# New places for the steps of every engine in a fused attention and mixture-of-experts kernel

## The chip, the cores and the metric

The kernel runs on one core of a Trainium2 chip. The time is that of the device, in microseconds (us), as the median of several executions. Matrix products run on TensorE (PE), whose weight loads have rows of their own (PEld); VectorE is DVE, ScalarE is ACT, GpSimd is POOL, and SP is the SyncE queue that issues nearly all DMAs. Everything is fp32.

## What is computed

Two results are added to the input `x` of 4 batches of 1024 tokens and 128 channels. The first is a power attention with 16 query heads over 8 key and value heads of size 64: squared scores take the place of the exponential, with a decay by token.

```python
q = _rope(qkvg[..., :hq*d]); k = _rope(...); v = ...
log_G = jnp.repeat(jnp.cumsum(jax.nn.log_sigmoid(6.906768 + gate), axis=1), 2, axis=2)
logits = 2 * jnp.log(jnp.abs(s) + 1e-30) + log_G[:, :, :, None] - log_G[:, :, None, :]
logits = jnp.where(tril, logits, -inf); a = jnp.exp(logits - logits.max(-1))
y = a @ v / (a.sum(-1) + 1e-6); y = layernorm(y, over d) * ln_w; out = y @ w_proj
```

The second is a layer norm followed by a router with 7 experts (the best two of each token, 366 places for each expert), a shared feed-forward network of width 512 for all tokens, and the experts' networks on the gathered tokens, added back with their weights.

## The kernel before

The work is cut into 32 pairs: 4 batches times 8 key heads, each with its two query heads. A pair has ten score steps (`STEPS`), in four diagonal units w = 0 to 3 (`ORDER` = 0, 2, 1, 3) of 256 columns. A score step is a set of PE products into two banks of PSUM (L778); DVE scales the diagonal ones with a masked decay block (`diagonal`, L1361), ACT squares the others (L964), DVE takes the running maximum over keys (`maximum`, here "top": L1380, L1390, L1392, L1397), ACT weighs the blocks (L960) and PE multiplies with the values (L811). Expert pairs are 9, 12, 15, ..., 27; there the gathered tokens of one expert run through up (PE, L614/L617 or their kin), gate and down.

No engine decides its order at run time. Each order is written out by tables:

- `*_FIRST` for the setup: a row (kind, at, by, then, na, nb) stands for na x nb items, item (a, b) at the tick at + by * a + then * b; `spread` (L89) sorts them.
- `*_AT` for the steady loop: a row (tick, kind, i) is placed in each pair p at T0 + 20 * p + tick if `wanted` (L133) allows it; `agenda` (L152) sorts them. A negative tick therefore lies before the pair, beside the work of the pair ahead. Scatters, loads and stores have tables of their own (`SCATTER_AT` and others).

Ticks are no times: they only fix which instruction follows which on an engine. What an engine waits for is fixed by semaphores at each step and does not depend on the tables. `jobs_of` (L179) hands PE's side jobs out in batches of five score steps: scores first, then transposes (`FLIPS`), then the other side jobs, then the value products. `bank_plan` (L185) walks through that order and gives each job the PSUM bank that has been taken least recently.

The steps that follow are named by kind:

- DVE setup: norm (layer norm), `forget` (the logarithms of the decay gates and their sums), `route` (L1162 to L1264: choice of the two experts, places, weights; among them the prefix sums of the experts' counts by doubling shifts, L1208 copy and L1209 add), gate (L1280, product of silu and the second up product), add (L1285).
- DVE loop: scale, top, fold (L1406, L1408: the maximum over the key blocks), sum (L1415, L1417), var (L1422, L1424), root (L1432 to L1440: an inverse square root by thirteen small steps), sup and sdn (L1318, L1326: the shared network of the last two units of tokens, in pair 31), wp (L1313: projection added to acc).
- POOL: `k` and `q` (`rotate`, L1502 and L1505, the rotation of keys and queries, after SP's swap of halves), `vs` (`scale_values`, L1516: values times decay, for the units w = 1, 2, 3 of the pair with 256, 128 and 384 columns; the trace calls the first two U and the third VS), `select` (L1524: masks the decay block), `scatter` (L1534, an indirect DMA), `combine` (L1544), n1 (L1570) and n2 (L1574), which divide and norm the outputs.
- ACT: decay (L882: the decay block that select masks), square, weigh, k, q and v copies (L897, L892, L905), y (L912), fin (L918), nt (L975), ysq (L985), silu (L844), e1 (L864: the exponential of the router), ht (L838).
- SP: swapk and swapq (L473), row (L448), keys (L491), rows (L502), weights (L455 to L462), sload (L521).

The exponential of e1 and the silu of the shared network use different tables of ACT, so going from one to the other takes an ACT_TABLE_LOAD. Here are the routing's last steps on DVE; the step behind e1 waits for it, and `gk` releases the scatters on POOL.

```python
v.tensor_tensor(e1, M12[:, 1], M12[:, 0], ALU.subtract).then_inc(v_e1, 1)   # L1251
yield
ve.wait_ge(a_e1, 1)
chain(v.tensor_scalar(e2, e1, 1.0, None, ALU.add))
...
v.tensor_tensor(gk[:, :], e1, keep[:, 32:64], ALU.mult).then_inc(v_gk, 1)   # L1264
```

Of the kernel before, what the change touches and what calls it, by code (L numbers as in the profile page):

```python
# [1639 lines left out]
```

## Time and profile before

| | us |
|---|---|
| median of 3 runs | 1023.90 |
| lowest and highest | 1023.67, 1024.99 |
| profiled execution | 1027.59 |
| its span | 1025.50 |
| PE busy in the span | 964.1 (94%) |
| DVE busy | 881.6 (86%) |
| ACT busy | 678.0 (66%) |
| POOL busy | 628.7 (61%) |

The busy time of an engine is the time in which it works, not in which it waits. The windows view cuts the span into stretches and gives each engine's busy time there. In the timeline view a row is an instruction (or some of one kind in a row); the bracket at its end says how long the engine had been idle and what ended that. PE does 8871 matmuls, DVE 1730 instructions, ACT 1078 and POOL 593.

### The profile page before, as it was taken

To read this page: it belongs to the slowest core of one execution; us is meant where nothing else is said; L and a number is where in the kernel's file an instruction comes from. 1 tells how busy PE (TensorE), PEld (TensorE's weight loads), DVE (VectorE), ACT (ScalarE), POOL (GpSimd) and SP (SyncE) were. 2 spreads that over 40 slices of the span, in tenths; PEclk is the share of its full clock that TensorE was granted. 3 is DMA by queue.
4 is the path that set the end of the run, shared out by engine and by line. 5 is a ranking of instruction groups with operands and counts; after the bars stand their busy time and mean duration, and the time that the engine had idled before them with its cause. 6 is when DMAs were issued, how large, how long until landed. Compare 5 with 4: busy or idle time off the path is not lost.

```text
span 1025.5 us, 23347 instructions
## 1 busy us (share of the span) xinstructions
PE 964.1 (94%) x8871; PEld 709.2 (69%) x8871; DVE 881.6 (86%) x1730; ACT 678.0 (66%) x1078; POOL 628.7 (61%) x593
## 2 busy tenths in 40 slices
PE   3999788989898999999999999999999999999977
PEld 2675466666676767676777686777677777767755
DVE  5668759999999988999998998899898989899983
ACT  2243466757667667868777868777876867786731
POOL 0320568898989775657567575748566747665611
PEclk9999989999999999999999999999999999999999
DMA  9301225443434343445354454345345435444550
GB/s 268 97 1 47 57 80 135 100 119 89 119 87 103 97 128 90 104 120 126 84 132 119 104 135 118 94 121 132 81 117 127 111 92 132 98 103 102 136 143 21
DMA packets 78767, 109.44 MB, mean 107 GB/s; under 512 B 15901, under 2 KB 47005, under 8 KB 78528
## 3 DMA queue, kind: packets, MB, share of 16 engines
q1 hardware_dynamic: 73584, 105.28, 39.3%
q0 software_dynamic: 5072, 2.67, 1.9%
q8 instruction: 70, 1.15, 0.5%
q14 instruction: 41, 0.34, 0.1%
HBM read 32.40 MB, written 11.36 MB: 43 GB/s over the span
## 4 chain that ended last, share of the span: by engine, by line
PE 71%; DVE 15%; POOL 4%; issue 4%; ACT 3%; DMA 1%; SPq 1%; DVEq 0%; POOLq 0%; ACTq 0%
PE PS L778 20%; PE PS L571 19%; PE PS L811 17%; PE PS L566 6%; DVE PS L1397 2%; PE PS L614 2%; DVE PS L1390 2%; PE PS L617 2%; DVE U L1397 2%; PE PS L624 1%; POOL xe_d L1534 1%; POOL U L1502 1%; DVE SM L1422 1%; PE PS L587 1%; DVE PS L1392 1%
## 5 line engine op out<-in xcount | busy, mean ns | idle before, releaser
L778 PE MATMUL PS<-Qt,Kt 64*128 64x256 f32 (+1 forms) x2560 | 281.0, 369 | 21.0 <-POOL Qt L1505 12.8
L778 PEld LDWEIGHTS PS<-Qt,Kt 64*128 64x128 f32 x2560 | 232.0, 190 | 62.3 <-POOL Qt L1505 14.7
L964 ACT ACTIVATE U<-PS 128x1024 f32<-128x1024 f32 x144 | 141.3, 1023 | 70.7 <-PE PS L778 59.4
L1502 POOL TENSOR_TENSOR U<-U,consts 128x512 f32<-128x512 f32 x96 | 127.3, 1326 | 45.6 <-DMA U<-U 45.5
L811 PE MATMUL PS<-U 128*64 128x256 f32 (+1 forms) x1344 | 141.2, 349 | 0.2 <-ACT U L960 0.2
L811 PEld LDWEIGHTS PS<-U 128*64 128x64 f32 x1344 | 94.0, 137 | 40.4 <-issue 6.0
L1524 POOL TENSOR_SCALAR_AFFINE_SELECT U<-U 128x256 f32<-128x256 f32 x128 | 59.9, 545 | 99.7 <-ACT U L882 99.4
L1570 POOL TENSOR_TENSOR U<-U,SM 128x1024 f32<-128x1024 f32 x32 | 71.7, 2241 | 73.5 <-DVE SM L1417 72.7
L1361 DVE SCALAR_TENSOR_TENSOR U<-PS,U 128x768 f32<-128x768 f32 x96 | 88.6, 953 | 30.8 <-PE PS L778 29.0
L1397 DVE SCALAR_TENSOR_TENSOR PS<-U,ES,PS 128x512 f32<-128x512 f32 x144 | 108.3, 752 | 4.7
L882 ACT ACTIVATE U<-U,negG 128x256 f32<-128x256 f32 (+1 forms) x256 | 98.7, 454 | 9.0 <-DMA U<-H_d 8.2
L1574 POOL TENSOR_TENSOR U<-U,SM 128x1024 f32<-128x1024 f32 x32 | 61.8, 1932 | 60.9 <-DVE SM L1440 60.8
L571 PE MATMUL PS<-XT,W 128*64 128x512 f32 x384 | 94.1, 603 | 0.0
L960 ACT ACTIVATE U<-U 128x768 f32<-128x768 f32 x96 | 81.2, 847 | 16.9 <-DVE U L1361 16.9
L1505 POOL TENSOR_TENSOR Qt<-Qt,U 128x512 f32<-128x512 f32 x64 | 83.6, 1307 | 9.2
L1534 POOL DMA_INDIRECT xe_d<-U,idx_s x64 | 70.1, 1096 | 21.7 <-issue 12.4
L566 PE MATMUL PS<-consts,U 128*128 128x128 f32 x533 | 78.5, 281 | 5.2 <-DVE U L1361 4.1
L566 PEld LDWEIGHTS PS<-consts,U 128*128 128x128 f32 x533 | 58.9, 142 | 20.9 <-issue 11.4
L892 ACT ACTIVATE U<-PS 128x512 f32<-128x512 f32 x64 | 38.1, 597 | 47.7 <-PE PS L571 47.7
L811 PE MATMUL PS<-U,VS 128*64 128x256 f32 x576 | 68.8, 379 | 0.1
L985 ACT ACTIVATE U<-U 128x1008 f32<-128x1008 f32 x32 | 33.4, 1043 | 49.3 <-PE PS L571 25.3
L571 PE MATMUL PS<-Wp,U 128*64 128x128 f32 x1024 | 58.9, 273 | 4.9 <-ACT U L918 4.9
(189 smaller groups left out, 1896.9 us busy)
## 6 DMA issues: line engine op xcount, KB each, us to landing
G<-U SPq DMA_DIRECT2D x512, 64.0 KB
U<-U SPq DMA_DIRECT2D x192, 128.0 KB
U<-H_d SPq DMA_DIRECT2D x32, 512.0 KB
Kt<-Kt SPq DMA_DIRECT2D x32, 256.0 KB
U<-in_w SPq DMA_DIRECT2D x21, 256.0 KB
acc<-in_x SPq DMA_DIRECT2D x4, 512.0 KB, 5.8
ye_d<-G SPq DMA_DIRECT2D x4, 512.0 KB, 7.3
U<-ye_d SPq DMA_DIRECT2D x4, 512.0 KB, 5.2
```

The lines of the kernel that those rows point to most:

```text
L566: return te.transpose(to, src, ident)
L571: mm = te.matmul(to[lo:lo + 64], weights[:, lo:lo + 64], moving, start=start, stop=stop)
L778: mm = te.matmul(bank[:, 256 * n:256 * n + 256 - lo], Kt[u % 2][(ki + hd) % 2][rows, 128 * j:128 * j + 128], Qt[p % 2][m // 2][rows, 256 * ...
L811: mm = te.matmul(P[4][64 * hd:64 * hd + 64, c + lo:c + 256], vt, A[s % NA][:, o:o + 256 - lo], start=begins and n == 0, stop=ends and n == 1)
L882: ex = s.activation(D[un % 3][:, lo:hi], HR[:, 256 * m + 128 * k2:256 * m + 256], ACT.Exp, scale=0.5, bias=negG[:, n:n + 1])
L960: s.activation(a_, a_, ACT.Square).then_inc(a_sd, 1)
L964: s.activation(A[n % NA], PS[:, first:first + 1024], ACT.Square, scale=0.125, bias=GUARD).then_inc(a_so, 1)
L1361: v.scalar_tensor_tensor(A[s % NA].rearrange("p (a t) -> p a t", a=2)[:, :, 0:384], PS[:, first:first + 1024].rearrange("p (a t) -> p a t" ...
L1397: v.scalar_tensor_tensor(run if i == m and n == 1 else PRUN, a_[:, :, n], es, PRUN, ALU.mult, ALU.max).then_inc(v_mx, 1)
L1502: g.tensor_tensor(sw, sw, sinT[:, cols], ALU.mult).then_inc(made, 1)
L1505: g.tensor_tensor(to, to, sw, ALU.add).then_inc(added, 1)
L1534: g.indirect_dma_start(xe_d[:, :], bass.IndirectOffsetOnAxis(ap=idx_s[:, c:c + 1], axis=0), hn_v[:, k], None, bounds_check=NE * SLOT - 1, ...
```

## The change

The tables `PE_FIRST`, `ACT_FIRST`, `DVE_FIRST`, `POOL_FIRST`, `PE_AT`, `ACT_AT`, `DVE_AT`, `POOL_AT` and `SP_AT` get new ticks. No instruction, wait, tile or size changes, and `SCATTER_AT`, `GATES_AT`, `LOAD_AT`, `ADD_AT` and `STORE_AT` stay. Through `bank_plan` 16 of 728 bank choices change. Sorted, the new tables differ from the old ones in this:

- POOL loop: vs1 goes from between vs3 and the rotations to right before vs2, in 31 pairs. Before: select3, vs3, vs1, k1, q0, combine or scatter, n1, q1, vs2, three selects, k0, n2. After: select3, vs3, k1, q0, combine or scatter, n1, q1, vs1, vs2, three selects, k0, n2. One scatter or combine goes before q0 in some pairs.
- ACT loop: decay3 behind weigh1 and v1's copy, nt0 before weigh2, in 32 pairs; ysq of pair 31 behind sup4.
- DVE loop: up6 before q0 in seven expert pairs, sup4 before the last root step of pair 31, else as before.
- SP loop: rows2 before keys in 15 pairs, weights0 behind rows2 and swapk, load 3 before rows(31,0), sload behind rows(31,1).
- PE loop: down before k0 and k1 in three expert pairs; in the tail sup8 earlier, sdn0 before sup14, sup15 behind the fins of pair 31, wp(15,0) before sdn1.
- Setup: on PE ht(0,0) before gate(0,1), cn behind v1, q0 behind down(4,1), q1 behind up(5,3); on ACT v0 before k1, silu(5,3) before e1; on DVE norms earlier among the gates, k0 behind step 12 of route, k1 and add(3) behind step 18, inside the prefix sums of the counts, gate(5,1) from before L1245 to behind it; on POOL vs(0,0) behind the two selects.

The diff's entries that these lines name, one to a line; the rest are left out:

```diff
 PE_FIRST = [
-    ('ht', 32.16, 28.14, 5.08, 4, 2),
+    ('ht', 31.98, 28.12, 5.08, 4, 2),
-    ('rt', 41.4, 27.8, 1.12, 4, 2),
+    ('rt', 40.86, 26.97, 0.83, 4, 2),
-    ('up', 33.04, 24.16, 6.2, 6, 4),
+    ('up', 32.15, 24.16, 7.29, 6, 4),
-    ('cn', 162.68, 0, 0, 1, 1),
+    ('cn', 163.91, 0, 0, 1, 1),
-    ('k', 147.14, 4.08, 0, 2, 1),
+    ('k', 149.42, 2.73, 0, 2, 1),
-    ('q', 167.45, 4, 0, 2, 1),
+    ('q', 171.58, 11.09, 2.19, 2, 1),
-    ('v', 159.28, 4.43, 0, 2, 1),
+    ('v', 158.39, 2.35, 0.57, 2, 1),
...
 ACT_FIRST = [
-    ('ht', 37.33, 28.36, 3.36, 4, 2),
+    ('ht', 35.41, 28.36, 3.36, 4, 2),
-    ('silu', 39.95, 23.79, 6.11, 6, 4),
+    ('silu', 39.95, 23.67, 6.11, 6, 4),
-    ('e1', 172.32, 0, 0, 1, 1),
+    ('e1', 181.04, 0, 0, 1, 1),
-    ('k', 151.74, 4.33, 0, 2, 1),
+    ('k', 153.39, 4.33, 1.27, 2, 1),
-    ('v', 163.14, 3.92, 0, 2, 1),
+    ('v', 157.07, 2.57, 0, 2, 1),
...
 DVE_FIRST = [
-    ('norm', 4.77, 29.15, 0.82, 4, 30),
+    ('norm', 3.71, 24.39, 0.82, 4, 30),
-    ('gate', 39.97, 24.16, 6.28, 6, 4),
+    ('gate', 40.64, 24.16, 6.28, 6, 4),
-    ('add', 83.46, 24.04, 0, 6, 1),
+    ('add', 88.41, 24.22, 0.17, 6, 1),
-    ('forget', 117.51, 0.77, 0, 44, 1),
+    ('forget', 119.82, 0.77, 0, 44, 1),
-    ('route', 149.17, 0.64, 0, 52, 1),
+    ('route', 149.17, 0.64, 0.1, 52, 1),
-    ('k', 153.48, 3.98, 0, 2, 1),
+    ('k', 156.88, 3.98, 0, 2, 1),
-    ('q', 187.97, 4.31, 0, 2, 1),
+    ('q', 180.15, 4.23, 0, 2, 1),
...
 POOL_FIRST = [
-    ('select', 294.1, 6.18, 0, 2, 1),
+    ('select', 254.64, 7.09, 1.48, 2, 1),
-    ('vs', 278.5, 0, 0, 1, 1),
+    ('vs', 275.84, 0, 0, 1, 1),
-    ('k', 159.29, 8.22, 0, 2, 1),
+    ('k', 151.2, 10.61, 0, 2, 1),
-    ('q', 232.63, 8.35, 0, 2, 1),
+    ('q', 237.21, 15.68, 3.36, 2, 1),
...
 PE_AT = [
-    (40.8, 'sup', 8),
+    (33.21, 'sup', 8),
-    (41.4, 'sup', 14),
+    (42.83, 'sup', 14),
-    (41.5, 'sup', 15),
+    (54.33, 'sup', 15),
-    (58.3, 'fin', 1),
+    (59.37, 'fin', 1),
-    (59.31, 'wp', 0),
+    (57.94, 'wp', 0),
-    (54.32, 'down', 0),
+    (50.37, 'down', 0),
...
 ACT_AT = [
-    (10.31, 'decay', 3),
+    (11.47, 'decay', 3),
-    (12.8, 'nt', 0),
+    (12.82, 'nt', 0),
-    (12.4, 'weigh', 2),
+    (13.04, 'weigh', 2),
...
 DVE_AT = [
-    (34, 'root', 0),
+    (33.41, 'root', 0),
-    (37.4, 'root', 2),
+    (37.07, 'root', 2),
-    (38.6, 'sdn', 0),
+    (39.28, 'sdn', 0),
-    (49.0, 'sdn', 1),
+    (40.49, 'sdn', 1),
...
 POOL_AT = [
-    (1.22, 'select', 3),
+    (0.1, 'select', 3),
-    (-16.1, 'vs', 1),
+    (-6.3, 'vs', 1),
-    (3.66, 'vs', 3),
+    (3.81, 'vs', 3),
-    (38.34, 'n2', 0),
+    (37.25, 'n2', 0),
-    (-15.9, 'k', 1),
+    (-15.04, 'k', 1),
-    (-15.66, 'q', 0),
+    (-13.54, 'q', 0),
...
 SP_AT = [
-    (9.68, 'rows', 2),
+    (7.9, 'rows', 2),
-    (-11.27, 'keys', 0),
+    (-12.05, 'keys', 0),
-    (-10.6, 'weights', 0),
+    (-7.61, 'weights', 0),
...
```

## Rows read from the trace of the kernel before

**Rows 1.** Windows view of five stretches, all engines: us and count; then clock, DMA share, GB/s.

```profile
0.00:21.90 21.90, 6.36 (x28) 5.59 (x28) 14.56 (x85) 3.28 (x5) 0.19 (x4) 1.00 0.96 267
21.90:131.50 109.60, 99.14 (x534) 65.64 (x534) 73.20 (x258) 41.44 (x65) 31.08 (x39) 0.98 0.22 57
131.50:375.00 243.50, 224.50 (x2081) 166.97 (x2083) 222.41 (x363) 161.68 (x260) 202.10 (x197) 0.97 0.41 105
375.00:950.00 575.00, 572.90 (x5726) 425.79 (x5724) 516.57 (x919) 439.42 (x702) 371.51 (x340) 1.00 0.44 112
950.00:1025.50 75.50, 61.17 (x508) 45.22 (x504) 54.83 (x107) 32.18 (x49) 23.80 (x17) 0.97 0.37 100
```

**Rows 2.** Timeline of the front: start, duration, engine, line; in brackets idleness and what ended it.

```profile
21.91 2.08 PE L614 MATMUL PS<-U 128*128 128x512 f32 x2 [0.87 <-ACT U L838]
```

**Rows 3.** Timeline of the setup's end, four engines.

```profile
102.03 0.59 ACT L905 ACTIVATE U<-PS 128x504 f32<-128x504 f32 x1 [2.15 <-PE PS L571]
...
103.33 1.27 POOL L1502 TENSOR_TENSOR U<-U,consts 128x512 f32<-128x512 f32 x1 [33.57 <-DMA U<-U]
103.39 1.73 DVE L1209 TENSOR_TENSOR U<-U 128x480 f32<-128x480 f32 x1
...
115.23 0.68 DVE L1280 TENSOR_TENSOR U<-U,PS 128x512 f32<-128x512 f32 x1
116.23 0.23 ACT L864 ACTIVATE SM<-SM 128x32 f32<-128x32 f32 x1 [3.86 <-DVE SM L1251]
116.48 1.28 ACT L844 ACT_TABLE_LOAD   x1
...
131.58 0.80 PE L778 MATMUL PS<-Qt,Kt 64*128 64x256 f32 x2 [6.36 <-POOL Qt L1505]
```

**Rows 4.** Timeline of DVE and POOL around 165, and one maximum at 222.

```profile
164.98 3.57 DVE L1390 SCALAR_TENSOR_TENSOR PS<-U,ES 128x512 f32<-128x512 f32 x1
...
165.34 0.85 POOL L1516 TENSOR_TENSOR VS<-U,ES 128x384 f32<-128x384 f32 x1
...
166.13 0.63 POOL L1516 TENSOR_TENSOR U<-U,ES 128x256 f32<-128x256 f32 x1
166.72 1.27 POOL L1502 TENSOR_TENSOR U<-U,consts 128x512 f32<-128x512 f32 x1
...
222.46 1.71 DVE L1390 SCALAR_TENSOR_TENSOR PS<-U,ES 128x512 f32<-128x512 f32 x1
```

**Rows 5.** Source view of L1390: ns min/median/max; L1397 of DVE's lines, 131.5 to 375.

```profile
L1390 DVE SCALAR_TENSOR_TENSOR PS<-U,ES x64: 696/746/3569, 142.3 to 977.2; 128x512 f32<-128x512 f32 x64
...
L1397 DVE SCALAR_TENSOR_TENSOR PS<-U,ES,PS 128x512 f32<-128x512 f32 x41 | 30.9, 753 | 1.6
```

**Rows 6.** Timeline of ACT, POOL and DVE around select3 and top1 of pair 2.

```profile
189.14 0.79 ACT L882 ACTIVATE U<-U,negG 128x256 f32<-128x256 f32 x2
...
189.83 0.58 ACT L905 ACTIVATE U<-PS 128x504 f32<-128x504 f32 x1
...
190.01 0.50 POOL L1524 TENSOR_SCALAR_AFFINE_SELECT U<-U 128x256 f32<-128x256 f32 x1 [0.95 <-ACT U L882]
...
190.30 0.84 ACT L960 ACTIVATE AX<-AX 128x768 f32<-128x768 f32 x1
...
191.57 1.77 DVE L1390 SCALAR_TENSOR_TENSOR PS<-U,ES,AX 128x512 f32<-128x512 f32 x1
```

**Rows 7.** Timeline of decay and select, in a K rotation's pair and in an expert's pair.

```profile
214.70 0.79 ACT L882 ACTIVATE U<-U,negG 128x256 f32<-128x256 f32 x2
...
217.57 0.42 POOL L1524 TENSOR_SCALAR_AFFINE_SELECT U<-U 128x256 f32<-128x256 f32 x1
...
458.49 0.51 POOL L1524 TENSOR_SCALAR_AFFINE_SELECT U<-U 128x256 f32<-128x256 f32 x1 [4.18 <-ACT U L882]
```

**Rows 8.** Timeline of PE in the tail.

```profile
1008.27 1.12 PE L731 MATMUL PS<-U 128*128 128x512 f32 x2 [1.55 <-DVE Kt L1318]
1009.23 3.73 PE L738 MATMUL PS<-U 128*128 128x128 f32 x32
```

More of the change, by code:

```diff
@@ L75 @@
[L75 to L78 removed]
+PE_FIRST = [('xt', 21.68, 28.07, 6.34, 4, 2), ('gate', 31.08, 28, 0.97, 4, 2), ('ht', 31.98, 28.12, 5.08, 4, 2), ('rt', 40.86, 26.97, 0.83, 4, 2), ('up', 32.15, 24.16, 7.29, 6, 4), ('down', 67.63, 24.55, 4.33, 6, 2), ('wv', 128.05, 0, 0, 1, 1), ('wpe', 142.49, 1, 0, 2, 1), ('cs', 133.52, 0, 0, 1, 1), ('hc', 144.08, 0, 0, 1, 1), ('tt', 153.19, 0, 0, 1, 1), ('cn', 163.91, 0, 0, 1, 1), ('k', 149.42, 2.73, 0, 2, 1), ('q', 171.58, 11.09, 2.19, 2, 1), ('v', 158.39, 2.35, 0.57, 2, 1)]
@@ new lines @@
+ACT_FIRST = [('xt', 16.06, 32.53, 3.82, 4, 2), ('ht', 35.41, 28.36, 3.36, 4, 2), ('silu', 39.95, 23.67, 6.11, 6, 4), ('wv', 145.37, 0, 0, 1, 1), ('wp', 146.82, 0.53, 0, 2, 1), ('ex', 122.53, 0, 0, 1, 1), ('hs', 156.67, 0, 0, 1, 1), ('es', 164.56, 0, 0, 1, 1), ('e1', 181.04, 0, 0, 1, 1), ('k', 153.39, 4.33, 1.27, 2, 1), ('q', 197.1, 4.58, 0, 2, 1), ('v', 157.07, 2.57, 0, 2, 1)]
+DVE_FIRST = [('norm', 3.71, 24.39, 0.82, 4, 30), ('gate', 40.64, 24.16, 6.28, 6, 4), ('add', 88.41, 24.22, 0.17, 6, 1), ('hl', 80.04, 0, 0, 1, 1), ('one', 112.96, 0, 0, 1, 1), ('forget', 119.82, 0.77, 0, 44, 1), ('logits', 127.34, 0, 0, 1, 1), ('route', 149.17, 0.64, 0.1, 52, 1), ('k', 156.88, 3.98, 0, 2, 1), ('q', 180.15, 4.23, 0, 2, 1)]
@@ new lines @@
+ACT_AT = [(31.7, 'sup', 0), (31.8, 'sup', 1), (31.9, 'sup', 2), (32.0, 'sup', 3), (42.3, 'sup', 4), (43.9, 'sup', 5), (44.0, 'sup', 6), (44.1, 'sup', 7), (12.82, 'nt', 0), (27.64, 'nt', 1), (-3.54, 'decay', 0), (-3.53, 'decay', 1), (5.5, 'decay', 2), (11.47, 'decay', 3), (23.4, 'y', 0), (31.69, 'y', 1), (54.54, 'fin', 0), (55.63, 'fin', 1), (43.3, 'ysq', 0), (9.08, 'xe', 0), (17.69, 'up', 0), (23.77, 'up', 1), (25.18, 'up', 2), (43.94, 'up', 3), (61.0, 'down', 0), (-22.94, 'k', 0), (-20.85, 'k', 1), (-10.3, 'q', 0), (-10.17, 'q', 1), (-9.65, 'v', 0), (10.31, 'v', 1), (5.74, 'square', 0), (6.97, 'square', 1), (13.39, 'square', 2), (13.44, 'square', 3), (13.8, 'square', 4), (13.89, 'square', 5), (7.78, 'weigh', 0), (10.73, 'weigh', 1), (13.04, 'weigh', 2), (15.23, 'weigh', 3)]
@@ new lines @@
+DVE_AT = [(27.0, 'sup', 0), (27.1, 'sup', 1), (27.2, 'sup', 2), (27.3, 'sup', 3), (36.53, 'sup', 4), (38.0, 'sup', 5), (38.1, 'sup', 6), (38.2, 'sup', 7), (39.28, 'sdn', 0), (40.49, 'sdn', 1), (23.72, 'fold', 0), (27.44, 'max', 0), (49.5, 'wp', 0), (54.28, 'wp', 1), (27.63, 'sum', 0), (32.03, 'var', 0), (33.41, 'root', 0), (34.29, 'root', 1), (37.07, 'root', 2), (28.36, 'up', 4), (33.13, 'up', 5), (41.26, 'up', 6), (43.61, 'up', 7), (-29.97, 'k', 0), (-27.97, 'k', 1), (-18.22, 'q', 0), (-16.07, 'q', 1), (-1.12, 'scale', 0), (-0.75, 'scale', 1), (-0.64, 'scale', 2), (4.39, 'scale', 3), (0.06, 'top', 0), (4.37, 'top', 1), (5.3, 'top', 2), (5.41, 'top', 3), (8, 'top', 4), (8.93, 'top', 5), (11.87, 'top', 6)]
```

34 lines of the change are left out of this document (4 added, 30 removed), and 9 rows, old and new, of tables (ACT_FIRST, PE_AT, PE_FIRST).

## The prediction

> **What bounds the kernel now.** I read the windows view first, cut where the work changes its kind [rows 1]. In the middle stretch, 375 to 950 us, TensorE (PE) is busy 572.90 of 575.00 us: nothing that the other engines win there can shorten it. In the last 75.50 us PE has 61.17, in the 109.60 us of the setup 99.14. The stretch from 131.50 to 375 is different: PE has 224.50 of 243.50 us, VectorE (DVE) 222.41, GpSimd (POOL) 202.10. There DVE and POOL both stand near the end of their time, and PE pays for both with 19 us of idleness. So the change can earn in three places: 131.5 to 375, the tail, and the setup. Then I read the stretches' own timelines. The setup ends on a chain: PE's router product, DVE's prefix sums and the routing steps, one exponential on ScalarE (ACT), DVE's last step, six scatters and the q rotation on POOL, first scores at 131.58 after 6.36 us of PE idleness [rows 3]. The tail ends on PE with one hole of 1.55 us [rows 8].
>
> The named cause is visible. L1390, DVE's diagonal maximum from two SBUF operands, takes 746 ns in the median and up to 3569 ns [rows 5]; the neighbouring L1397, which has one operand in PSUM, has a mean of 753 ns over 41 instructions in the same stretch [rows 5]. The longest one starts at 164.98 and lasts until 168.55, over POOL's VS product (0.85), vs1 (the U product at 166.13, ends 166.76) and L1502 (ends 167.99) [rows 4]. I went through DVE's instructions of 131.5 to 375 and took from each the usual duration of its form: 24.9 us are left over, 10.1 of them on nine L1390 (three of them in [rows 4, 6]), 3.5 on six L1380, the rest on root's and the sums' small steps and on fold. The same sum for 375 to 960 is 26.3 us, and there it is free.
>
> **The change part by part.** Sorting both sets of tables gives the two orders of each engine; I go through what differs. Waits and instructions are the same.
>
> 1. Front of PE: ht(0,0) now comes before gate(0,1), so ACT's step L838 has a PE product to hide behind. Before, L614 waited 0.87 us for it [rows 2]. The second product was issued anyway. -0.87 us up to PE's tt, which releases the prefix sums.
>
> 2. DVE's prefix sums of the routing counts (L1208/L1209) now carry k1 and add(3) among them, which stood elsewhere: two steps of 128x512 at 0.68 us each (the row at 115.23 [rows 3] is such a step), spaced at 0.6: +1.28. The sums collide with POOL's K rotation: L1209 takes 1.73 us at 103.39 beside L1502, which starts at 103.33 [rows 3], and I add up 3.3 us of such stretching to 109.8. On ACT the v0 copy (before at 102.03, 0.59 us [rows 3]) now stands before k1's, 0.60: k1's ends at about 102.03 - 0.87 + 0.59 + 0.60 = 102.35. Before, 4.5 us of swap and landing lay between that copy and the rotation, so the rotation starts near 106.8, when fewer prefix steps are left: I estimate 2.35 us of stretching (1 to 4). Part 2 is +1.28 - 0.95 = +0.33.
>
> 3. e1, ACT's exponential of the router (L864), now stands behind silu(5,3). Before it ran at 116.23 and the table load for silu, 1.28 us, came after it [rows 3]. Now silu(5,3) has to wait for its PE product and for DVE's gate(5,1), which moves from before L1245 to after it; the nearest row is the gate at 115.23, ending 115.91 [rows 3]. In the clock of before: silu starts at 115.2 to 115.5, takes 0.60, then load 1.28, then e1 0.23: it ends at 117.3 instead of 116.46, +0.9. The lower end is 0 (silu ready before e1's operand is and the load done in the wait), the upper end is +2.6: silu(5,3) waits for gate(5,1) at the end of DVE's queue, a further 1.7. I take +0.9, since the gate is one step from where it was. DVE's k0 moves behind the twelfth routing step, on the same chain: +0.6. The six scatters and two q rotations behind it are unchanged. Parts 1 to 3 are -0.87 + 0.33 + 0.9 + 0.6 = **+0.95** (-0.5 to +3.2).
>
> 4. decay3 of ACT moves behind weigh1 and the v copy. In pair 2 the chain ran decay 0.79 us at 189.14, v copy 0.58, weigh 0.84, and POOL's select had waited 0.95 us for that decay [rows 6]. Behind both, select3 starts 1.1 us later (the v copy already overlaps in part), and pairs 0 to 2 have no slack for it; but vs1 is out of POOL's way in front of it, 0.63 us. On the later pairs there is slack: in a pair with a K rotation the decay ends at 215.49 and select starts at 217.57, 2.1 us later, and in the PE-bound part POOL waits 4.18 us for the decay that it could lose [rows 7]. For pairs 0 to 2: **+0.2** (0 to +1.1). In return weigh1 and the maximum top1 behind it come 0.69 us earlier at 191.57 where DVE's start hung on ACT; I give that -0.4.
>
> 5. The main part: vs1 leaves its place behind VS and goes to the run vs1, vs2, select, select, select before n2, in 31 pairs. (a) What it frees: top1 collided with VS and U one after the other: 3.57 at 164.98, 1.77 at 191.57 [rows 6] and once more so at a third place, against 0.75: 2.82 + 1.02 + 1.03 = 4.9 us, of which the vs1 share is what goes (0.6 each where VS alone still holds it): -1.6. In the intervals with a K rotation q0 and q1 of POOL start 0.35 earlier with vs1 gone, and L1390 at 222.46 with 1.71 us, 0.97 too long [rows 4], meets L1505 less or not at all: three such, -0.35 each, -1.05. (b) What it costs: vs1 now runs beside DVE's root, thirteen steps of 0.2 us each, as part of a POOL run of 0.63 (vs1), a smaller product for vs2 and 2 x 0.5 us (selects) without a gap [rows 4, 6]. A step that falls into it waits for the rest of it. The nine or ten pairs of the stretch: in two of nine the root is under way at that time, so 0.62 x 2 = 1.3 (0 to 0.62 x 9 = 5.6). The sum is -1.6 - 1.05 + 1.3 - 0.4 (from 4) = **-1.75** (-7.5 to +4). The low end is all of L1390's 10.1 us freed with 2.6 paid back elsewhere.
>
> Here a rule of the Trainium skill bears. The rows show that one DVE instruction outlasts one POOL instruction beside it: the 3.57 us at 164.98 spans three [rows 4]. The Trainium skill, "SBUF — State Buffer", section "Who interferes with whom", says that a two-input DVE instruction in SBUF and a reading GpSimd instruction take the port pair for a whole instruction each, by order of issue. By that the instruction would wait for one and run, 0.85 + 0.75 = 1.6 us, part 5 (a) would lose its -1.6 for vs1, and the sum would be 1023.3; the trace disagrees at 164.98.
>
> 6. The SP queue, nt0 before weigh2, ysq31, expert downs before k: at nothing. Nearly all of it lies in 375 to 950, where PE has 2.1 us of idleness in all [rows 1]; what covers them is PE's own queue. If that cover were gone, nt0 ahead of weigh2 would cost a copy of about 0.6 us per pair, as the v copy of 0.58 [rows 6].
>
> 7. Tail: before, PE waits 1.55 us at 1008.27 for a bank that DVE's L1318 frees, with the 32 matmuls of sdn, 3.73 us, right behind [rows 8]. After, sdn(0) stands before sup14, so it fills the hole. The two wp products at the end wait for ACT's fin for 0.1 to 0.35 us, as wp(15,0) now precedes sdn(1). **-1.6** (-2 to -1). Next late would be DVE's last add, which keeps its 0.69 us.
>
> **The sum.** Profiled execution before: 1027.59 us (span 1025.50), 3.69 above the median 1023.90 of the runs. +0.95 + 0.2 - 1.75 - 1.6 = -2.2, so the profiled one would be 1025.4 and the median 1021.7. A change within 0.2%, 2.05 us, cannot be told from none in this kernel; the sum is just past that, at 1021.85.
>
> **The rivals.** B, no change: the loop's balance is zero, because what L1390 no longer meets the L1380, root and sum steps meet instead. For it: those already carry 14.8 of the 24.9 us. Against: the balance would have to be exact. 1023.9 + 0.95 + 0.2 - 1.6 = 1023.45.
> C, larger gain: the stretched L1390 vanish without being paid back: 10.1 us less 2.6 for root, and the tail: 1023.9 + 1.15 - 7.5 - 1.6 = 1015.95. For it: DVE has only 21 us of room in 243.50, so every microsecond it gets is PE's. Against: DVE's order in the loop is nearly the one it had, only POOL's is new; the L1390 beside L1505 (three places) and n1 are not moved far.
> D, slower: the run of four POOL instructions in front of n2 holds the root in each of nine pairs. n2 waits for root, the fin and the next pair's sums come late. Price: 5.6 - 1.05 - 0.4 instead of 1.3 - 3.05: the loop at +4.15; 1023.9 + 1.15 + 4.15 - 1.6 = 1027.6. It decides from a leftover of DVE in 131.5 to 375 above 28 us (24.9, and 2.9 more make the whole slower by 2.05). For it: the four are back to back by their ticks, and POOL is at 83% of the stretch. Against: in most pairs root is later than select.
> E, the change does not do what it says: the sum of POOL-stretched DVE time stays within 1 us of 24.9, and only setup and tail move. It gives 1023.45 as B does and shares its chance.
> The rule that a DVE step is held by one POOL instruction at most gives B too, since then the removed vs1 frees nothing; [rows 4] speaks against it, and that is why B has not more. It is the Trainium skill's, named above.
>
> **How the numbers follow.** Forecast 42%, of it 28 faster than 1021.85 and 14 within; B with E 20%, all within; C 17%, all faster; D 21%, all slower. Faster 45%, same 34%, slower 21%. The forecast's own range is 1019.5 to 1023. The whole range goes down to 1014.5, past C's 1015.95 by the spread of its parts, and up to 1027.5, which takes in half of D: some 1.5 in 10 are left out. It has to be wide, since the bounds of part 5 alone are 11.5 us apart.
>
> **What would show it.** First scores at 132.3 to 132.7 instead of 131.58 (parts 1 to 3); e1 after 117. In 131.5 to 375: no L1390 above 2.5 us, DVE's leftover near 22, PE's busy time the same in a stretch shorter by 1.5 to 2. From 375 to 950 the same time and the same PE share. No hole at sup14. It would be wrong if the first scores come after 134 or before 130.5, if the stretch moves by more than 4 us, or if PE opens holes in 375 to 950.

## The result, and the profile after

The changed kernel takes 1035.89 us in the median (1035.72 to 1037.22, 4 runs), the kernel before beside it 1024.44. The ratio is 1.0114 with a 95% interval of 1.0097 to 1.0132: slower by 10 to 13.5 us, where 2.2 us less had been forecast.

The line numbers of the changed kernel are 30 lower than before (L1390 is L1360, L778 is L748). In the runs that follow they are lower by as much as their tables are shorter: by 3 in `h1_combine1_only` and `h2_q0_only`, by 12 in `e1_setup_only` and `h3_setup_e1_back`, by 14 in `g2_tail_only`, by 30 in `f1_all_but_decay`. The windows view of both kernels follows, cut at the same places of the work (first scores, fold of pair 8, pair 30): the columns are span of the stretch, then busy time and count of PE, PE loads, DVE, ACT and POOL, clock, DMA share, GB/s. The changed kernel:

```profile
0.00:21.90 21.90, 7.13 (x30) 6.25 (x31) 17.67 (x105) 3.25 (x4) 0.19 (x4) 1.00 0.96 258
21.90:133.50 111.60, 99.07 (x534) 65.28 (x532) 68.59 (x239) 38.59 (x63) 31.18 (x39) 0.98 0.23 57
133.50:385.70 252.20, 227.27 (x2111) 168.39 (x2113) 226.31 (x366) 163.61 (x263) 201.85 (x196) 0.97 0.40 102
385.70:970.00 584.30, 579.37 (x5774) 428.05 (x5770) 524.32 (x931) 446.62 (x712) 373.53 (x343) 1.00 0.45 112
970.00:1033.50 63.50, 51.48 (x428) 37.59 (x428) 45.86 (x92) 24.12 (x35) 15.35 (x13) 1.00 0.37 100
```

And the kernel before, the last three stretches cut to match (the first two are [rows 1]):

```profile
131.50:377.30 245.80, 226.80 (x2111) 168.76 (x2113) 224.26 (x366) 163.72 (x264) 203.03 (x198) 0.97 0.41 104
377.30:960.00 582.70, 579.03 (x5776) 430.13 (x5772) 523.96 (x932) 445.49 (x711) 379.53 (x345) 1.00 0.44 112
960.00:1025.50 65.50, 52.74 (x428) 39.08 (x428) 45.59 (x92) 24.07 (x35) 14.84 (x11) 0.97 0.35 97
```

PE does the same work in nearly the same busy time in each; only in the tail the same 428 matmuls take 51.48 us instead of 52.74, at a granted clock of 1.00 instead of 0.97. The setup is 2.0 us longer, pairs 0 to 8 are 6.4 us longer, the long PE-bound part 1.6, and the tail is 2.0 shorter: 8.0 in all, as the spans say (1033.5 and 1025.5). The medians are 11.45 apart, because the profiled execution of before was itself 3.15 above the median of 1024.44; nine other traces with the old setup reach fold of pair 0 at 161.98 to 164.44 us, eight of them before its 163.68.

The end of the setup in the changed kernel, to be held beside [rows 3]:

```profile
116.13 0.18 DVE L1221 TENSOR_TENSOR SM<-SM 128x32 f32<-128x32 f32 x1
116.28 0.60 ACT L814 ACTIVATE U<-PS 128x512 f32<-128x512 f32 x1 [3.58 <-PE PS L584]
116.89 1.28 ACT L834 ACT_TABLE_LOAD   x1
118.19 0.23 ACT L834 ACTIVATE SM<-SM 128x32 f32<-128x32 f32 x1
118.45 0.18 DVE L1224 TENSOR_SCALAR SM<-SM 128x32 f32<-128x32 f32 x1 [2.14 <-ACT SM L834]
...
133.53 0.80 PE L748 MATMUL PS<-Qt,Kt 64*128 64x256 f32 x2 [5.69 <-POOL Qt L1475]
```

DVE had the router's difference ready (L1221) only 0.12 us later than before, 116.13 against 116.01. The exponential then came at 118.19 instead of 116.23 [rows 3], behind a silu that waited 3.58 us for its PE product and behind the table load. Scatters, rotations and first scores follow: 133.53 against 131.58.

The waits view for POOL's select in the two kernels, before first (sum in us, how often, longest):

```profile
POOL U L1524 <- ACT U L882: 99.4, 41, 6.8
```

```profile
POOL U L1494 <- ACT U L852: 141.0, 44, 7.6
```

And the source view of the diagonal maximum (min/median/max ns), which answers to [rows 5]:

```profile
L1360 DVE SCALAR_TENSOR_TENSOR PS<-U,ES x64: 696/754/2332, 143.6 to 987.6; 128x512 f32<-128x512 f32 x64
L1360 DVE SCALAR_TENSOR_TENSOR PS<-AX,ES x16: 697/760/2490, 152.7 to 933.5; 128x512 f32<-128x512 f32 x16
```

The 3569 ns of this form are gone, as the change wanted; over all four forms of the line the longest is 2490 ns in the changed kernel. But the sum that I made before, of DVE time above the usual of each form, is 26.3 us in 133.5 to 385.7 where it was 24.9 in the matching stretch: as much stretching, in other places.

### The profile page after: what moved, and what is told of

It is laid out like the page before. It is cut to its first block, busy times and chain, and to the rows that moved or that the text cites. A ratio compares the mean times of both kernels' runs of the same rounds, so it can differ in the third digit from the quotient of the medians.

```text
span 1033.5 us, 23345 instructions
## 1 busy us (share of the span) xinstructions
PE 964.3 (93%) x8871; PEld 705.6 (68%) x8871; DVE 882.7 (85%) x1730; ACT 676.2 (65%) x1076; POOL 622.1 (60%) x593
## 4 chain that ended last, share of the span: by engine, by line
PE 61%; DVE 19%; POOL 6%; issue 6%; DMA 3%; ACT 2%; SPq 2%; POOLq 0%; DVEq 0%; ACTq 0%
PE PS L541 16%; PE PS L748 16%; PE PS L781 14%; PE PS L536 5%; DVE PS L1367 3%; DVE PS L1360 3%; POOL xe_d L1504 2%; PE PS L584 2%; DVE U L1367 2%; PE PS L587 2%; PE PS L594 2%; POOL U L1472 1%; SPq L472 1%; DMA G<-U 1%; DVE SM L1392 1%
## 5 line engine op out<-in xcount | busy, mean ns | idle before, releaser
L748 PE MATMUL PS<-Qt,Kt 64*128 64x256 f32 (+1 forms) x2560 | 282.7, 371 | 26.7 <-POOL Qt L1475 17.1
L748 PEld LDWEIGHTS PS<-Qt,Kt 64*128 64x128 f32 x2560 | 230.7, 191 | 71.0 <-POOL Qt L1475 19.0
L1472 POOL TENSOR_TENSOR U<-U,consts 128x512 f32<-128x512 f32 x96 | 131.9, 1374 | 53.9 <-DMA U<-U 53.6
L1494 POOL TENSOR_SCALAR_AFFINE_SELECT U<-U 128x256 f32<-128x256 f32 x128 | 65.4, 589 | 141.2 <-ACT U L852 141.0
L1331 DVE SCALAR_TENSOR_TENSOR U<-PS,U 128x768 f32<-128x768 f32 x96 | 88.3, 952 | 30.6 <-PE PS L748 30.4
L1360 DVE SCALAR_TENSOR_TENSOR PS<-U,ES 128x512 f32<-128x512 f32 x64 | 62.0, 969 | 4.6 <-DMA G<-U 1.1
```

Of the source, the lines that this page charges most:

```text
L748: mm = te.matmul(bank[:, 256 * n:256 * n + 256 - lo], Kt[u % 2][(ki + hd) % 2][rows, 128 * j:128 * j + 128], Qt[p % 2][m // 2][rows, 256 * ...
L1331: v.scalar_tensor_tensor(A[s % NA].rearrange("p (a t) -> p a t", a=2)[:, :, 0:384], PS[:, first:first + 1024].rearrange("p (a t) -> p a t" ...
L1360: v.scalar_tensor_tensor(PRUN, a_[:, :, 0], es, diag[:, :, 0], ALU.mult, ALU.max).then_inc(v_mx, 1)
L1472: g.tensor_tensor(sw, sw, sinT[:, cols], ALU.mult).then_inc(made, 1)
```

## The experiments

Gains and losses are ratios to the kernel before, run on the same chip in the same session (medians of it 1023.6 to 1025.9). One per mille is 1.02 us. Changed kernel and experiments ran on several chips, so what "comes back" is a difference of two such ratios and is uncertain by 2 to 3.5 us. Where the clock time of a step matters I compare the start of fold (L1408), one per pair, between traces, as a difference to its value in pair 0 or another pair of the same trace.

**Tables and ticks one by one, on the kernel before.** All four setup tables as in the diff ahead (`e1_setup_only`), the whole new `SP_AT` (`e4_sp_only`), and two single ticks:

```diff
 POOL_AT:                                 # e2_vs1_only
-    (-16.1, 'vs', 1)
+    (-6.3, 'vs', 1)
 ACT_AT:                                  # e3_decay_only
-    (10.31, 'decay', 3)
+    (11.47, 'decay', 3)
```

> The kernel before with the four new setup tables (PE_FIRST, ACT_FIRST, DVE_FIRST, POOL_FIRST) and the old loop. Theory A (the setup gives its own share: the first scores of the changed kernel came at 133.53 instead of 131.58 us): +2 us over the kernel before, first scores near 133.5, and the loop keeps its spacing of pairs. Rival B (a setup that ends otherwise changes the alignment of DVE and POOL in the loop, so the loop loses too): +5 us or more, fold of pair 7 more than 4 us late.

Measured: 1.0028 (1.0015 to 1.0041), so +2.9 us. First scores at 134.07, and from fold of pair 0 to fold of pair 31 it loses nothing (829.24 us against 829.99). Theory A.

> The kernel before with one tick changed: vs1 on POOL from -16.1 to -6.3, so right before vs2, in 31 pairs. Theory A (vs1 isn't the cause of the loss; it frees the diagonal maximum of one collision and meets root instead, net near nothing): within 1.5 us of the kernel before. Rival B (the longer run of POOL instructions beside root, my case D): +4 us or more, root's steps stretched by 3 us more in 131 to 375.

Measured: 1.0001 (0.998 to 1.0022). The folds fall behind by 2.7 us from pair 0 to 6, and by pair 10 most of that is made up (0.8 left). Theory A.

> The kernel before with one tick changed: decay 3 on ACT from 10.31 to 11.47, behind weigh1 and the v copy, in 32 pairs. Theory A (the late decay is the loss of the loop: POOL's waits for it in the changed kernel doubled from 10.6 to 21.6 us over pairs 0 to 8, so POOL's whole queue behind select3 is late there): +4 to +6 us, folds of pairs 0 to 6 falling behind by 0.6 to 1 us each. Rival B (slack hides it, as I predicted): within 0.5 us, +0.2.

Measured: 1.0011 (0.9994 to 1.0029). From pair 0 to 5 it loses 1.9 us, by pair 10 it has 0.5 left. Theory A falls as a cause of the whole. B's 0.2 us lies within the interval of the total, but not in the early pairs.

> The kernel before with the new SP_AT, SP's queue of DMA issues in the loop (rows2 before keys, weights0 later). Theory A (SP's order is the loss: rows2 waits for the maxima of its unit, and the copy of the keys waits behind it, so first scores of K pairs wait): +3 us or more, all in pairs with new keys. Rival B (free, as I predicted): within 0.5 us.

Measured: 1.0007 (0.9991 to 1.0023), the folds never more than 0.3 us behind. Theory B.

None of these carries the loss of the loop. The next four take one part out of the changed kernel instead.

**One part taken back in the changed kernel.**

```diff
 ACT_AT:                                  # f1_all_but_decay
-    (11.47, 'decay', 3)
+    (10.31, 'decay', 3)
```

The others take back a whole table: `POOL_AT` (`f2_all_but_pool`), `PE_AT` (`f3_all_but_pe`), the four setup tables (`f4_loop_only`).

> The changed kernel with one tick back: decay 3 on ACT at 10.31 again, before the v copy and weigh1. Theory A (late decay together with the new order of POOL is the loss: select3 now stands directly behind n2 and one scatter, so POOL idles 2 to 3.5 us in front of it in each of pairs 1 to 8, where alone in the old order the idle time was 1.7 to 3.1 with other work moved into it): the changed kernel gets back 4 to 6 of its 11.5 us, so +6 over the kernel before, and fold of pair 7 some 3 us after the old one instead of 8.4. Rival B (the banks and PE's order make the loss): it stays at +10 or more.

Measured: 1.0168 (1.0144 to 1.0193): +17 us. Taking the late decay back makes the changed kernel slower by 5 to 6 us. Both theories fall, and this run turned out to be the key: what it loses more than the changed kernel is in pairs 15, 21 and 27 (fold of pair 15 loses 1.8, of 21 loses 3.4, of 27 loses 1.8; in the changed kernel -0.2, -0.4 and 0.2), three pairs behind the expert pairs 12, 18 and 24, where the combines of an expert are.

> The changed kernel with the old POOL_AT. Theory A (POOL's order is part of the loss: one more scatter of 1.3 us before q0 in seven pairs, vs1 beside root): 2 to 4 us of the 11.5 come back. Rival B (late decay alone carries the loop's loss, whatever POOL's order): under 1 us comes back.

Measured: 1.0047 (1.0033 to 1.0061): 6.3 of the 11.5 us come back. Theory A, by more than it said. The folds lose 1.0 us from pair 0 to 9, where the changed kernel loses 6.1: most of what POOL's table costs lies there.

> The changed kernel with the old PE_AT, so the old bank choices in the loop and the old tail. The trace of the changed kernel has waits of scores for DVE's projection add (4.2 us, three times, pairs 4, 6, 8) that the kernel before has not. Theory A (they are real losses that the new PE order makes): 3 to 4 us come back in the loop, 1.6 to 2 are lost again in the tail, so about +9.5. Rival B (the waits only show that DVE is late for other reasons): the loop stays, the tail's loss makes it +13.

Measured: 1.0086 (1.0066 to 1.0107), +10 in the median, near A's sum and below B's; its folds stay within 0.2 us of the changed kernel's from pair 2 to 7. The waits for DVE's add stay, so they are not made by PE's order or its banks. So the loop does as B says, and B's loss in the tail isn't to be seen in the median. Why the total is as low as A's stays open.

> The changed kernel with the four old setup tables. Theory A (parts add up: the new setup alone gave +2.9): +8.5 over the kernel before. Rival B (the late setup makes the loop worse by alignment): +4 or less.

Measured: 1.0074 (1.0055 to 1.0094), +8.1 in the median. Theory A: parts of setup and loop add up.

**POOL's table.** The whole of it on the kernel before (`e5_pool_only`), and single ticks taken back in the changed kernel:

```diff
 POOL_AT:                                 # f6_all_but_vs1
-    (-6.3, 'vs', 1)
+    (-16.1, 'vs', 1)
 POOL_AT:                                 # g1_all_but_q0
-    (-13.54, 'q', 0)
+    (-15.66, 'q', 0)
```

> The kernel before with the whole new POOL_AT. Taking the new POOL_AT out of the changed kernel gave back 6.4 of its 11.5 us. Theory A (POOL's new order is worth its loss by itself, a scatter ahead of q0 and vs1 ahead of vs2): +5 to +6.5 us, folds of pairs 0 to 6 late by 4 us and not made up after. Rival B (it is a loss only together with the other new orders, as vs1 alone gave only +1): +1 to +2 us, mostly made up by pair 10 as in the run with vs1 alone.

Measured: 1.0101 (1.0072 to 1.013), more than either theory, and nearer A. The folds lose 3.8 us in pairs 0 to 7 and then 1.8 each at pairs 15, 21 and 27, which A did not say.

> The changed kernel with one tick back: vs1 at -16.1. Theory A (vs1 beside root is the harmful part of POOL's order, since n2 and with it everything behind it on POOL comes later): 4 to 6 of the 11.5 us come back. Rival B (the scatter ahead of q0 is the harmful part, or the late select3): under 1.5 us comes back.

Measured: 1.0101 (1.0071 to 1.0131): about 1 us comes back, within the uncertainty. Theory B. The move for which I had worked out most of my sum is not what costs.

> The changed kernel with one tick back: q0 of POOL at -15.66, so it has one scatter less ahead of it in seven pairs. Theory A (vs1 is the harmful part): under 1.5 us comes back. Rival B (the scatter, 1.0 us and 0.3 of issue, ahead of q0 is it, since first scores of a pair wait for the rotated queries): 4 to 6 of the 11.5 us come back.

Measured: 1.0066 (1.0044 to 1.0088): some 5 us come back. Theory B, so q0 is one cause. Its trace is of an execution 3.4 us above the median and doesn't show where they come back: its folds lose 6.0 us up to pair 7, as in the changed kernel.

**Two ticks of POOL alone, on the kernel before.**

```diff
 POOL_AT:                                 # h1_combine1_only
-    (66.52, 'combine', 1)
+    (62.5, 'combine', 1)
 POOL_AT:                                 # h2_q0_only
-    (-15.66, 'q', 0)
+    (-13.54, 'q', 0)
```

and the rest of `POOL_AT` without these two and vs1 (`h5_pool_rest`).

> The kernel before with one tick changed: combine 1 of POOL (an indirect DMA in the third pair behind each expert pair) from 66.52 to 62.5, so it stands ahead of vs3 and the rotations. In the run with the whole new POOL_AT vs3 and L1502 then fell onto the maximum L1390 of pairs 13 and 19 and others, 3.58 us instead of 0.74, and folds lost 0.8 to 1.8 us in pairs 12, 15, 21, 24 and 27. Theory A (that is combine 1 alone): +4 to +7 us, all of it behind pair 11. Rival B (it needs vs1's new place too, for vs3 ends earlier without it): under 1.5 us.

Measured: 1.011 (1.0078 to 1.0141), +10.4 us in the median from one tick. Theory A, and more. From fold 14 to 15 it loses 2.4 us, from 20 to 21 4.0, from 26 to 27 2.4. The timeline of this run in pair 15 (the expectation called it 13, a miscount), DVE and POOL, with PE's next hole:

```profile
535.64 0.67 POOL L1521 TENSOR_SCALAR_AFFINE_SELECT U<-U 128x256 f32<-128x256 f32 x1 [0.68 <-ACT U L879]
...
536.47 1.83 POOL L1541 DMA_INDIRECT ye_d<-U  x1 [0.16 <-issue]
...
537.38 4.16 DVE L1387 SCALAR_TENSOR_TENSOR PS<-AX,ES,U 128x512 f32<-128x512 f32 x1
537.76 1.42 POOL L1513 TENSOR_TENSOR VS<-U,ES 128x384 f32<-128x384 f32 x1
...
538.56 1.19 POOL L1513 TENSOR_TENSOR U<-U,ES 128x256 f32<-128x256 f32 x1
539.13 1.83 POOL L1499 TENSOR_TENSOR U<-U,consts 128x512 f32<-128x512 f32 x1
...
543.71 1.14 PE L775 MATMUL PS<-Qt,Kt 64*128 64x256 f32 x8 [2.12 <-DVE U L1358]
```

The same place in the kernel before:

```profile
538.94 1.27 POOL L1516 TENSOR_TENSOR VS<-U,ES 128x384 f32<-128x384 f32 x1
...
540.04 0.74 DVE L1390 SCALAR_TENSOR_TENSOR PS<-AX,ES,U 128x512 f32<-128x512 f32 x1
540.32 0.93 POOL L1516 TENSOR_TENSOR U<-U,ES 128x256 f32<-128x256 f32 x1
```

Before, no combine stands between select and VS. With the combine ahead of it, the maximum starts at 537.38 inside the combine (536.47 to 538.30), and behind that POOL's run of VS, vs1 and L1499 goes on without a gap until 540.96: the maximum takes 4.16 us and ends at 541.54. Scale (L1358) is late behind it, and PE, which has no slack at that place, stands for 2.12 us. The same 4.16 us come at 703.24 and 868.68, and PE's 2.12 at 709.57 and 875.01; at 457.17, 621.00, 788.49 and 952.47, inside the combines of the other experts, the maximum takes 2.36 to 2.38. There it waits for VS alone, though POOL's products follow without a gap just as well; now vs1 is the one that is held (1.65 us):

```profile
456.31 1.80 POOL L1541 DMA_INDIRECT ye_d<-U  x1 [0.20 <-issue]
457.17 2.38 DVE L1387 SCALAR_TENSOR_TENSOR PS<-U,ES 128x512 f32<-128x512 f32 x1
457.56 1.43 POOL L1513 TENSOR_TENSOR VS<-U,ES 128x384 f32<-128x384 f32 x1
458.36 1.65 POOL L1513 TENSOR_TENSOR U<-U,ES 128x256 f32<-128x256 f32 x1
459.89 1.33 POOL L1499 TENSOR_TENSOR U<-U,consts 128x512 f32<-128x512 f32 x1
```

So the wait is for one product at four places and for three at the other three, and no run tells what decides it. In the kernel before, the only maximum of the long kind is the one at 164.98 [rows 4], inside a scatter. DVE's time above the usual in 375 to 960 is 40.8 us in this run, 26.3 in the kernel before.

The changed kernel and `f1_all_but_decay` differ only in the tick of the decay. In f1, pair 15:

```profile
546.25 1.82 POOL L1514 DMA_INDIRECT ye_d<-U  x1 [0.16 <-issue]
547.15 3.58 DVE L1360 SCALAR_TENSOR_TENSOR PS<-AX,ES,U 128x512 f32<-128x512 f32 x1
547.53 1.41 POOL L1486 TENSOR_TENSOR VS<-U,ES 128x384 f32<-128x384 f32 x1
```

In the changed kernel:

```profile
548.43 0.41 POOL L1494 TENSOR_SCALAR_AFFINE_SELECT U<-U 128x256 f32<-128x256 f32 x1 [2.06 <-ACT U L852]
548.70 0.75 DVE L1360 SCALAR_TENSOR_TENSOR PS<-AX,ES,U 128x512 f32<-128x512 f32 x1
549.13 1.75 POOL L1514 DMA_INDIRECT ye_d<-U  x1 [0.30 <-issue]
...
550.35 1.41 POOL L1486 TENSOR_TENSOR VS<-U,ES 128x384 f32<-128x384 f32 x1
```

The late decay holds POOL for 2.06 us, so the maximum (548.70 to 549.45) starts ahead of the combine, is not held, and is over before VS starts at 550.35. The late decay and the early combine belong together: the decay is the guard of the maximum. That is why taking it back alone made things worse.

All twenty traces bear this out. With the early combine and the early decay (`h1_combine1_only`, `e5_pool_only`, f1) the folds lose 1.8 to 4.0 us at each of the pairs 15, 21 and 27. With the early combine and the late decay (the changed kernel, `f3_all_but_pe`, `f4_loop_only`, `f6_all_but_vs1`, `g1_all_but_q0`) they lose at most 0.3 there, as the kernels with the old combine do. So the 10.4 us of this tick alone are not part of what the changed kernel loses. What is left of it there is small: from pair 24 to 31 these five lose 2.0 to 3.3 us, the twelve with the old combine 0 to 1.5 (in each case against the trace of the kernel before). No run takes this tick back alone in the changed kernel.

The traces also tell what the combine itself does. In all of them together, 220 maxima overlap an indirect DMA of POOL and nothing else of POOL; none takes more than 0.79 us. One of them in the kernel before:

```profile
280.08 1.01 POOL L1534 DMA_INDIRECT xe_d<-U,idx_s  x1 [0.16 <-issue]
280.17 0.70 DVE L1390 SCALAR_TENSOR_TENSOR PS<-U,ES 128x512 f32<-128x512 f32 x1
```

And where a product of POOL starts 0.05 us or more behind the maximum, with no indirect DMA under way at the maximum's start, the maximum takes at most 0.76 us (460 places). It takes both for a wait of this kind: the maximum starts inside the DMA, and a product follows 0.34 to 0.40 us behind it. Even then it is sometimes the product that is held and not the maximum; what decides is not shown.

> The kernel before with one tick changed: q0 of POOL from -15.66 to -13.54, so one scatter stands ahead of it in seven pairs up to pair 8. Theory A (first scores wait for the queries longer): +2.5 to +4 us, all in pairs 1 to 8, kept afterwards. Rival B (the time is made up by pair 10, as with vs1 alone): under 1 us.

Measured: 1.0047 (1.0031 to 1.0063), +5 in the median. Theory A: the folds lose 3.6 us from pair 0 to 7 and about 1.1 of it comes back by pair 11. The run's POOL in pair 0 and one of PE's new waits:

```profile
144.29 0.62 POOL L1513 TENSOR_TENSOR U<-U,ES 128x256 f32<-128x256 f32 x1
145.08 1.01 POOL L1531 DMA_INDIRECT xe_d<-U,idx_s  x1 [0.17 <-issue]
146.12 1.28 POOL L1499 TENSOR_TENSOR U<-U,consts 128x512 f32<-128x512 f32 x1
...
293.75 2.23 PE L775 MATMUL PS<-Qt,Kt 64*128 64x256 f32 x24 [1.09 <-DVE acc L1310]
```

The scatter of 1.01 us takes a place where POOL before had waited 0.63 us for the swap, so q0 is late by the rest, 0.57 us when measured from the scatter ahead of VS, and the rotations meet more maxima (1.71 us each beside a rotation that begins 0.12 us earlier, at 230.15, 283.39 and 337.15, which the kernel before doesn't have): fifteen L1390 are stretched in the early stretch, by 15.5 us, where it had been nine by 10.1. All POOL-made stretching there is 29.3 us against 24.9. PE's scores then wait for DVE's add, 2.1 us in all in three places, where the kernel before has 0.2 in one; e5, g1 and the changed kernel have 3.2, 2.2 and 4.4. That the scatter costs the time is shown by the tick; that it does so through these stretched maxima is read from the trace and not tested by itself.

> The kernel before with the other new ticks of POOL_AT: select3, n2, k1, vs3, combine 0 and combine 2; q0, combine 1 and vs1 as before. They change the order in pairs 4 to 6 alone, by one scatter. Theory A: within 0.7 us. Rival B (they hold the part of POOL_AT's 9.6 us that combine 1 and q0 do not): +3 us or more.

Measured: 1.0012 (0.9998 to 1.0026). Between the two theories, nearer A: the folds lose 1.8 us from pair 3 to 4 and make up some 0.5 to 1.2 of it by pair 9.

**The setup.** The new setup tables with one row back:

```diff
 ACT_FIRST:                               # h3_setup_e1_back
-    ('e1', 181.04, 0, 0, 1, 1)
+    ('e1', 172.32, 0, 0, 1, 1)
```

> The run with the new setup alone, with one tick back: the router's exponential (e1) ahead of the last silu on ACT. Theory A (that exponential, which waited 2.14 us longer in the changed kernel, is the whole loss of the setup): first scores 1.8 us earlier than there, setup loss gone, within 0.7 us of the kernel before. Rival B (k1 and add 3 inside the prefix sums, and the K rotation that now meets the route steps, carry part of it): +1 to +2 us stay.

Measured: 1.0004 (0.9987 to 1.0021). Theory A. PE's first scores in the run with the new setup alone, then with the exponential back:

```profile
134.07 1.22 PE L766 MATMUL PS<-Qt,Kt 64*128 64x256 f32 x4 [5.45 <-POOL Qt L1493]
```

```profile
130.75 1.65 PE L766 MATMUL PS<-Qt,Kt 64*128 64x256 f32 x6 [6.08 <-POOL Qt L1493]
```

In the thirteen traces with the exponential ahead of the silu, old setup or new, the first scores come at 130.53 to 132.15, in the seven with it behind at 133.40 to 134.65. From the start of the step that makes its operand (L1251 in the kernel before) to that of the exponential it is 0.22 us in the first kind, 2.06 to 3.75 us in the second.

**The tail, the sum, and a best version.** Tail: only the ticks of sup and sdn in pair 31, on the kernel before (`g2_tail_only`); `h4_three_back` takes combine 1, q0 and e1 back in the changed kernel; `h6_setup_tail` joins the setup of h3 to the tail.

```diff
 PE_AT:                                   # g2_tail_only, the ones that reorder
-    (40.8, 'sup', 8)
+    (33.21, 'sup', 8)
...
-    (41.4, 'sup', 14)
+    (42.83, 'sup', 14)
-    (41.5, 'sup', 15)
+    (54.33, 'sup', 15)
```

> The kernel before with the new places of the shared network's last steps alone (sup and sdn on PE, ACT and DVE, all in pair 31). Theory A (the tail's part of my forecast): no PE hole of 1.55 us ahead of the last two up products, -1.6 us from fold of pair 31 to the end, so about -0.15% against the kernel before. Rival B (the hole moves to another wait): 0 within 0.5 us.

Measured: 0.9998 (0.9985 to 1.0011), not to be told from none. In the trace the hole is gone (PE in the tail, compare [rows 8]):

```profile
1004.13 3.73 PE L724 MATMUL PS<-U 128*128 128x128 f32 x32
1007.71 1.02 PE L717 MATMUL PS<-U 128*128 128x512 f32 x2
1008.57 1.04 PE L552 MATMUL PS<-consts,U 128*128 128x128 f32 x8
1009.44 1.02 PE L717 MATMUL PS<-U 128*128 128x512 f32 x2
```

and from fold of pair 31 to the end of the span it takes 30.4 us where the kernel before takes 31.8, with PE busy for 23.50 us in both. Over all traces that end takes 29.4 to 31.0 us with the new tail and 30.7 to 34.0 with PE's old one. The mechanism is shown; that it shortens the median isn't.

> The changed kernel with three entries back: combine 1 and q0 of POOL and the router's exponential of ACT's setup. Theory A (these three are the causes, and the rest of the change is worth little): 9 to 11 of the 11.5 us come back, so within 2 us of the kernel before. Rival B (the late decay and the late vs1 cost 3 us or more once the others are gone): +3 to +5 us.

Measured: 1.0034 (1.002 to 1.0048), +3.5 us: 8 of the 11.5 come back, which is B's size. The three together are the larger part of the cause, not the whole, and by the pairs 15, 21 and 27 above the combine has little share in it. In this trace the folds lose 3.4 us in pairs 0 to 7, with the late decay and the late vs1 in place. These two lost 1.9 and 2.7 us there alone and got most of it back afterwards. The run also keeps the other new ticks of POOL, PE, ACT, DVE and SP, so it doesn't show that the rest is theirs.

> The kernel before with the new setup tables, the router's exponential back ahead of the last silu, and the new places of sup and sdn in pair 31. Loop as before. Theory A (both parts are small gains: first scores at 130.75 instead of 131.58 us, and 1.5 us in the tail): -1.5 to -2.5 us against the kernel before, the fastest of all. Rival B (execution noise of the loop hides it): within 0.1%.

Measured: 0.9993 (0.998 to 1.0006). The fastest trace of all (span 1021.2), but not separable from the kernel before. Theory B.

## Why the prediction was wrong, step by step

Set against the stretches, the forecast was +0.95 for the setup, -1.55 for 131.5 to 375, nothing behind it and -1.6 for the tail. Measured were +2.0, +6.4, +1.6 and -2.0.

Part 1, the front: L614 starts at 20.73 to 20.89 us in the new setup instead of 21.91 [rows 2], even better than the 0.87. But the product that releases the prefix sums came at 100.49, later than the 99.94 of before, and over all traces the two setups overlap (98.55 to 100.05 for the old, 99.15 to 100.49 for the new). The gain is lost on the way; I had assumed that it carries through 80 us.

Part 2: k1 and add 3 cost what I took (0.6 each). The K rotation started at 108.19, not 106.8, and met the route steps instead of the prefix sums: L1185, a product of 0.69 us, takes 1.67. Up to L1221 the terms -0.87, +0.33 and +0.6 for k0 make 0.06 us late, and 0.12 was measured. That is luck: the product came 0.55 us late, and the way from it to L1221 was 0.43 shorter.

Part 3 was the term of the setup that was mis-sized: +0.9 forecast, 1.84 in this trace (2.06 instead of 0.22 between L1221 and the exponential), up to 3.5 in others, beyond the 2.6 that I gave as the upper end. I had the silu ready at 115.2 to 115.5. Its PE product (L584, up(5,3)) started at 115.11 and ended at 116.2, 0.1 us behind the gate, so PE's order set it; I took it from the clock of before, though PE's order around it had changed.

Part 4: "pairs 0 to 2, +0.2": wrong in place and size. Alone the late decay cost 1.9 us in pairs 0 to 5, and in the changed kernel select's wait was 141.0 us in all where it had been 99.4. I had read 2.1 us of slack from a pair with a K rotation [rows 7] and taken it for all later pairs. With the K rotation POOL still doesn't wait in the changed kernel (select at 221.78). In the pairs between it does. The same select before and in the changed kernel:

```profile
243.34 0.50 POOL L1524 TENSOR_SCALAR_AFFINE_SELECT U<-U 128x256 f32<-128x256 f32 x1
```

```profile
250.28 0.88 POOL L1494 TENSOR_SCALAR_AFFINE_SELECT U<-U 128x256 f32<-128x256 f32 x1 [3.46 <-ACT U L852]
```

At 304.90 it is 3.33 us once more.

Part 5 held the failed step. Its sum for 131.5 to 375, -1.75, prices vs1 and the maxima that it frees, and nothing else of POOL's order. Its named move was forecast at a small net and was small. The step that fails is that the other differences have no term, in part 5 or in part 6 ("at nothing"): they were put at nothing without a reason. My list of the change has them as one scatter or combine before q0 in some pairs. The scatter ahead of q0, in seven pairs, costs 5 us alone and gives some 5 back when it is taken out of the changed kernel; all of POOL's table gives back 6.3. The combine goes even ahead of vs3, which the list doesn't say. It costs 10 us alone, and in the changed kernel little, since the late decay stands in front of it; that was luck too, as I had seen neither. For the stretch from 375 on, the only cover that I named was that PE is the bound there, with 2.1 us of idleness. That is true of the kernel before; but DVE has 516.57 of 575.00 us there [rows 1], and a single instruction held for 3.4 us longer is more than the slack at its place. "PE-bound" was an average over 21 pairs, not a cover for each instant.

Part 7, the tail, was right: -1.6 forecast, -1.4 in the run with it alone. Of the -2.0 in the matched stretches, 1.26 us are PE's shorter busy time at the higher granted clock, so that number holds more than the new order of the steps.

The rivals: D named a slower end but with vs1 as its mechanism, and the run without vs1 refutes that. E said that the stretching stays the same within 1 us and only setup and tail move: the sum is 26.3 us for 24.9, a little outside, but the stretch itself grew by 6.4 us. So the stretched time of DVE in sum does not tell the cost; its place does.

The rule of the Trainium skill ("SBUF — State Buffer", "Who interferes with whom"), that the later one waits for a whole instruction of the other, agrees with the four maxima of 2.36 to 2.38 us in the run with the combine alone: each ends about 0.56 us behind VS. It disagrees in size with the three of 4.16 us against a usual 0.74, and with the one at 164.98: there it was three POOL products. Its other rule there, that the order of issue decides who is held, agrees where no indirect DMA is under way: in all twenty traces a product that starts 0.05 us or more behind the maximum leaves it alone. Inside an indirect DMA the starts in the trace don't follow it, since the maximum is held by a product that starts 0.34 to 0.40 us later.

What stays open: what holds the last 3.5 us, for which the late decay, the late vs1 and the rest of the new tables are all left; why the losses of decay or vs1 alone are made up by pair 10 and in the changed kernel are not; what decides whether a maximum that starts inside an indirect DMA is held, and for one product or for three.

## What to carry to other kernels

Price every instruction that changes its neighbour on a queue, also the two or three that seem side effects: here one scatter of about 1 us in front of a rotation cost more than the move the change was made for, and one indirect DMA of 1.83 us in front of a run of POOL products alone cost twice that, though in the changed kernel another tick happened to shield it. A single edit can be harmful alone and harmless beside another, so test it both ways: added to the old kernel and taken out of the new one. Where two engines hold each other up, what counts is whether the single long instruction of the one is issued before the other's run begins or inside it; read both start times in the trace (here 537.38 against 536.47, and 548.70 against 549.13 where it was not held) and ask of each edit which way it pushes them. And an engine that is the bound of a stretch on average covers a delay only up to the slack of the instruction that waits for it.
